# A four-layer graph network on one core: the first layer's softmax scaling moved to GpSimd, and a new order of its steps

## The chip, the core and the metric

The kernel runs on one core of a Trainium2 chip, as one launch. The metric is the device time of a launch in microseconds (us), lower is better. The core has five engines with an instruction queue of their own, which run side by side and wait for one another on semaphores: PE (TensorE, matrix multiplications and transposes, which write the PSUM banks), DVE (VectorE), ACT (ScalarE), POOL (GpSimd, which reads and writes SBUF alone) and SP (SyncE, which here only issues DMAs). Within a queue nothing overtakes: an instruction that waits holds up all that stand behind it.

## The reference

Four graph layers run one after the other over x (128 graphs of 64 nodes, 256 features), each followed by a residual and a layernorm. The change touches the first alone:

```python
    xp = jnp.einsum('mn,bnf->bmf', L_norm, x)
    h = xp @ Wc + bc
    h = _layernorm(h, g1, be1)
    h = jax.nn.relu(h)
    x1 = h + x
    q, k, v = x1 @ Wq, x1 @ Wk, x1 @ Wv          # 4 heads of 64
    scores = jnp.einsum('bhnd,bhmd->bhnm', q, k) / np.sqrt(hd)
    scores = jnp.where(adjacency[None, None] > 0, scores, -1e9)
    attn = jax.nn.softmax(scores, axis=-1)
    o = jnp.einsum('bhnm,bhmd->bhnd', attn, v) @ Wo + bo
    x2 = _layernorm(x1 + o, g2, be2)
    m = jax.nn.gelu(x2 @ W1 + b1) @ W2 + b2
    return _layernorm(x2 + m, g3, be3)
```

## The kernel before

The 8192 tokens are cut into groups of 256 (four graphs, two tiles of 128 rows). Four streams, numbered 0 to 3, work on four groups at a time, each with two PSUM banks and SBUF buffers of its own, and there are 8 turns of four groups. The work on one group is a chain of numbered slots that goes back and forth between the engines. A step is written s.n below: 3.11 is slot 11 of stream 3. A slot can have a part on more than one engine.

- 0 and 1: PE mixes the graph's nodes (L288), ACT copies, PE multiplies by Wc (L889); DVE adds the bias (L808) and takes layernorm statistics (L353, L357).
- 1 on POOL: reciprocal standard deviation (L365, L367). 2 on DVE: the layernorm's two passes (L395, L400), ReLU and residual (L815).
- 3: PE transposes (L921), ACT and DVE split the value in two (L675, L798). 4 and 5: PE makes q, k (24 matmuls of L332) and v (12 of L332), which ACT copies out (L678, L681, L684).
- 6: PE makes the scores (L952, L962), DVE their negated maximum (L819). 7: ACT takes the exponential (L688). 8: DVE sums (L823), takes the reciprocal (L825) and multiplies (L827).
- 9: PE transposes the weights (L969), ACT copies (L693). 10: PE weights v (L980), ACT copies (L696). 11: PE multiplies by Wo (L889), DVE adds the residual (L832) and takes statistics (L353, L357), POOL the reciprocal deviation (L365, L367). 12 on DVE: the two layernorm passes (L395, L400).
- 13 to 15 and 150: transposes (L921), the MLP up (L332), gelu on ACT (L705), down (L913), and DVE's add and statistics (L841). 16 on DVE: the third layernorm; 17 on DVE and POOL: statistics of the last one; 18: ACT applies it, SP stores.
- 3, 13 and 16 on POOL: a bias is added in four pieces of 128 x 128 each, by the helper at L301.

Which of these stands where in an engine's queue comes from a table written by hand, `plan0`: for each engine a tick for each slot, a period of 88 ticks, and for each stream a lead. The function `weave` walks the ticks of a period and issues what is due; it sets only the order, since the queues run as fast as their semaphores allow. In the profile's names PSUM is `ps`, most SBUF buffers lie in `H`, and PE's fp32 matmuls are counted twice (a product of 4 instructions is a row with x8, a transposition of 4 one with x4).

Of the kernel before, what the change touches and what calls it, by code (L numbers as in the profile page):

```python
# [21 lines left out]
ALU = mybir.AluOpType  # L22
# [5 lines left out]
P = 128  # L28
BATCH, NODES, D = 128, 64, 256
# [88 lines left out]
def build_program(nc, ctx, t, out_rows):  # L118
# [107 lines left out]
    bc, g1, be1, bo, g2, be2, b2, g3, be3 = (vec0[:, n, :] for n in range(9))  # L226
# [66 lines left out]
    PIECES = 4  # L293
# [54 lines left out]
    LN_STATS = 2 * TILES - 1  # L348
# [40 lines left out]
    LN_AFFINE = 2 * TILES  # L389
# [124 lines left out]
    def half_blocks(h):  # L514
# [2 lines left out]

    plan0 = dict(
        period=88, lead=(0, 12, 20, 32),
        pe={0: 13, 1: 20, 3: 29, 4: 36, 5: 40, 6: 45, 9: 59, 10: 60, 11: 67, 13: 75, 14: 82, 15: 89, 150: 91},  # L520
        act={0: 17, 3: 32, 4: 39, 5: 42, 7: 53, 9: 60, 10: 63, 13: 79, 14: 86, 18: 167, 140: 87},
        dve={1: 25, 2: 27, 3: 34, 6: 49, 8: 57, 11: 72, 12: 72, 13: 79, 15: 97, 16: 106, 17: 153},
        pool={1: 19, 3: 41, 11: 63, 13: 77, 15: 96, 16: 70, 17: 150},
        sp={2: 42, 4: 0, 18: 116})

    with nc.Block() as block:

# [50 lines left out]
        def _(pool):  # L578
# [11 lines left out]
            c = Chain(pool, pool_steps)  # L590
# [47 lines left out]
            def stage(s, slot, turn):  # L638
                for n, at in enumerate((1, 11)):
                    if slot == at:  # L640
                        ln_reciprocal(pool, steps.enter(s, slot, turn), s, var_ready[s], rstd_ready[s],
                                      2 * turn + n + 1)
                if slot == 15:
                    ln_reciprocal(pool, tail.enter(s, slot, turn), STREAMS + s, var2_ready[s], rstd2_ready[s],
                                  2 * turn + 3)
                if slot == 17:
                    ln_reciprocal_and_shift(pool, tail.enter(s, slot, turn), STREAMS + s, var2_ready[s],
                                            rstd2_ready[s], 2 * turn + 4)
                if slot == 3:
# [63 lines left out]
        def _(dve):  # L713
# [69 lines left out]
            for k in range(KD):  # L783
# [2 lines left out]
            dve.sem_inc(late_made, 1)  # L786
            dve.wait_ge(w0_loaded, 16 * 16)

            steps = Steps(dve, "l0_dve", {1: 1 + LN_STATS, 2: LN_AFFINE, 8: 2, 11: 1 + LN_STATS,
                                          12: LN_AFFINE - 1})  # L790
            tail = Steps(dve, "l0_dve_tail", {15: 1 + LN_STATS, 16: LN_AFFINE - 1, 17: LN_STATS})
            ahead(dve, var2_ready, by=2)
# [8 lines left out]
            def stage(s, slot, turn):  # L801
                c = (steps if slot < 15 else tail).enter(s, slot, turn)
                for n, (at, h) in enumerate(((3, 0), (13, 1))):
                    if slot == at:
                        split_lo(s, FM * turn + n + 1, h)
                if slot == 1:
                    dve.wait_ge(product_done[s], 3 * turn + 1)
                    c.step(dve.tensor_tensor(hb_t[s], token_major(s, 1), over_tiles(bc), ALU.add))  # L808
                    c.settle()
                    ln_statistics(dve, c, hb_t[s], s, var_ready[s])  # L810
                if slot == 2:
                    c.step(ln_affine(dve, c, hb_t[s], s, g1, lambda n: be1, var_ready[s], rstd_ready[s], 2 * turn + 1))
                    c.settle()
                    dve.wait_ge(xs_loaded[s], 16 * turn + 16)
                    dve.scalar_tensor_tensor(out=x1_t[s], in0=hb_t[s], scalar=0.0, in1=xs_t[s],  # L815
                                             op0=ALU.max, op1=ALU.add).then_inc(x_ready[s], 1)
                if slot == 6:
                    dve.wait_ge(sc_done[s], turn + 1)
                    dve.tensor_reduce(sm_max[:, s, :].rearrange("p (b c) -> p b c", b=2), score_blocks(s), AX_X,  # L819
                                      ALU.max, negate=True).then_inc(sc_ready[s], 1)  # L820
                if slot == 8:
                    dve.wait_ge(exp_ready[s], turn + 1)
                    c.step(dve.tensor_reduce(sm_sum[:, s, :], attn[s], AX_X, ALU.add))  # L823
                    c.settle()
                    c.step(dve.reciprocal(sm_inv[:, s, :], sm_sum[:, s, :]))  # L825
                    c.settle()
                    dve.tensor_tensor(attn[s], attn[s], sm_inv[:, s, :].unsqueeze(2).to_broadcast([P, 2 * NJ, NODES]),  # L827
                                      ALU.mult).then_inc(at_ready[s], 1)
                if slot == 11:
                    dve.wait_ge(product_done[s], 3 * turn + 2)  # L830
                    dve.wait_ge(biased_ready[s], 2 * turn + 1)
                    c.step(dve.tensor_tensor(hb_t[s], token_major(s, 0), x1b_t[s], ALU.add))  # L832
                    c.settle()
                    ln_statistics(dve, c, hb_t[s], s, var_ready[s])
                if slot == 12:
                    ln_affine(dve, c, hb_t[s], s, g2, lambda n: be2, var_ready[s], rstd_ready[s], 2 * turn + 2)\
                        .then_inc(x_ready[s], 1)
                if slot == 15:
                    dve.wait_ge(product_done[s], 3 * turn + 3)
                    dve.wait_ge(biased_ready[s], 2 * turn + 2)  # L840
                    c.step(dve.tensor_tensor(y_t[s], token_major(s, 0), x2b_t[s], ALU.add))  # L841
                    c.settle()
                    ln_statistics(dve, c, y_t[s], STREAMS + s, var2_ready[s])
                if slot == 16:
                    dve.wait_ge(xb_ready[s], turn + 1)
                    ln_affine(dve, c, y_t[s], STREAMS + s, g3, lambda n: xr0_t[s][:, n, :], var2_ready[s],
                              rstd2_ready[s], 2 * turn + 1, 2 * turn + 3).then_inc(y_made[s], 1)
                if slot == 17:
                    dve.wait_ge(y_made[s], turn + 2)
                    ln_statistics(dve, c, y_t[s], STREAMS + s, var2_ready[s])  # L850
                (steps if slot < 15 else tail).leave(s, slot)
# [1141 lines left out]
```

## Time and profile before

| | us |
|---|---|
| median of 3 runs | 2195.67 (2194.35 to 2195.98) |
| the profiled execution, its own time | 2193.9 |
| its span | 2192.0 |
| a turn of the first layer, steady | 72.96 |
| PE busy in that turn | 72.58 |
| DVE / ACT / POOL busy in that turn | 63.28 / 37.81 / 42.14 |

The first layer takes about the first 640 us of the span. Its loop begins at 32.8 us and PE's last matmul in it ends at 626.1 us; the next layer's first starts at 645.9 us. The time outside the span (1.9 us) is launch and end. A row of the timeline gives start, duration, engine, line, operation, output and input, and in brackets how long the engine had stood idle and for whom.

### The profile page before, as it was taken

What the parts mean: (1) busy time and instruction counts of PE and PEld (TensorE: products, weight loads), DVE (VectorE), ACT (ScalarE), POOL (GpSimd) and SP (SyncE); (2) the same over time, 40 slices, a digit from 0 to 9 for tenths busy, and PEclk for the clock granted to TensorE, in tenths of its full rate; (3) what the DMA queues carried; (4) which work ended last, traced back from release to release, by engine and by line L of the source; (5) the groups of instructions that cost most, each with busy time, mean ns of one, the idle gap of its engine ahead of it and who ended that gap; (6) DMA issues with size and microseconds to landing.
All of it is one profiled execution on the core that took longest, in us unless ns stands there. A gap on an engine that the chain in (4) does not pass through costs nothing. (4 is left out here: it accounts for less than half of the span.)

```text
span 2192.0 us, 44070 instructions
## 1 busy us (share of the span) xinstructions
PE 2105.3 (96%) x17941; PEld 1843.1 (84%) x17941; DVE 1368.7 (62%) x2737; ACT 1158.0 (53%) x2184; POOL 472.8 (22%) x1131
## 2 busy tenths in 40 slices
PE   6999999999969989999999999999999999899998
PEld 4899889988959978888888999988888799777886
DVE  5788888888866644433334443353444488876775
ACT  1554465445534457644445444353443477657987
POOL 3555565556530000000000000000000122003343
PEclk9999999999989999999999999999999999999999
DMA  4001211121131110000000000000000143001333
GB/s 128 16 21 50 59 36 35 49 59 37 36 109 58 57 51 20 1 20 1 1 1 20 20 1 1 1 0 20 1 1 1 47 125 121 1 20 45 83 88 78
DMA packets 77074, 82.99 MB, mean 38 GB/s; under 512 B 7136, under 2 KB 74592, under 8 KB 76000
## 3 DMA queue, kind: packets, MB, share of 16 engines
q1 hardware_dynamic: 76896, 80.53, 12.4%
q8 instruction: 122, 2.00, 0.4%
q14 instruction: 56, 0.46, 0.1%
HBM read 55.34 MB, written 25.17 MB: 37 GB/s over the span
## 5 line engine op out<-in xcount | busy, mean ns | idle before, releaser
L332 PE MATMUL ps<-R 128*128 128x256 f32 (+3 forms) x8136 | 1489.9, 343 | 12.1 <-DVE R L1461 7.4
L332 PEld LDWEIGHTS ps<-R 128*128 128x128 f32 x8136 | 1308.6, 190 | 169.6 <-issue 7.5
L1407 ACT ACTIVATE late_half<-ps,lstm_bias 128x512 f32<-128x512 f32 (+2 forms) x460 | 283.0, 669 | 375.3 <-PE ps L332 375.3
L374 POOL TENSOR_TENSOR ln_veps<-ln_mv,eps_tile 128x2 f32<-128x2 f32 x128 | 24.9, 195 | 1179.2 <-DVE ln_mv L357 1179.2
L301 POOL TENSOR_TENSOR H<-H 128x128 f32<-128x128 f32 x384 | 203.8, 563 | 1.4 <-DMA residual<-H 1.4
L1477 DVE TENSOR_TENSOR late_half<-late_half 128x1024 f32<-128x1024 f32 (+2 forms) x32 | 37.6, 1176 | 183.6 <-ACT late_half L1407 183.6
L1401 ACT ACTIVATE late_half<-late_half 128x1024 f32<-128x1024 f32 (+2 forms) x66 | 68.1, 1031 | 125.0 <-DVE late_half L1482 78.5
L889 PE MATMUL ps<-H 128*128 128x256 f32 x512 | 125.3, 388 | 0.8 <-ACT H L672 0.8
L913 PE MATMUL ps<-H 128*128 128x256 f32 x512 | 120.3, 380 | 0.0
L1479 DVE TENSOR_TENSOR late_half<-late_half 128x1024 f32<-128x1024 f32 (+2 forms) x32 | 37.6, 1176 | 131.1 <-ACT late_half L1407 131.1
L400 DVE SCALAR_TENSOR_TENSOR H<-H,ln_rstd 128x256 f32<-128x256 f32 x192 | 99.3, 557 | 13.4 <-POOL ln_rstd L367 11.4
L889 PEld LDWEIGHTS ps<-H 128*128 128x128 f32 x512 | 94.5, 194 | 12.3 <-ACT H L672 1.0
L913 PEld LDWEIGHTS ps<-H 128*128 128x128 f32 x512 | 94.7, 190 | 12.0
L1489 DVE TENSOR_TENSOR H<-late_half 128x1024 f32<-128x1024 f32 (+2 forms) x34 | 45.9, 1350 | 89.8 <-ACT late_half L1407 89.8
L353 DVE BATCH_NORM_STATS2 ln_stats<-H 128x6 f32<-128x256 f32 x256 | 95.8, 415 | 3.3
L1461 DVE TENSOR_TENSOR R<-H,R 128x1024 fp32r<-128x1024 f32 (+2 forms) x66 | 95.7, 1451 | 1.3 <-ACT R L1380 1.1
L1380 ACT ACTIVATE R<-H 128x1024 fp32r<-128x1024 f32 (+2 forms) x66 | 94.4, 1431 | 0.0
L395 DVE SCALAR_TENSOR_TENSOR H<-H,ln_mv 128x256 f32<-128x256 f32 x192 | 90.1, 509 | 1.6
L377 POOL TENSOR_TENSOR ln_rstd<-ln_veps,minus_half 128x2 f32<-128x2 f32 x128 | 88.5, 692 | 10.0
L1492 DVE TENSOR_TENSOR late_half<-late_half 128x1024 f32<-128x1024 f32 (+2 forms) x32 | 37.6, 1176 | 80.8 <-ACT late_half L1407 80.8
L1475 DVE TENSOR_TENSOR late_half<-late_half 128x1024 f32<-128x1024 f32 (+2 forms) x34 | 40.9, 1202 | 58.6 <-ACT late_half L1407 58.6
L357 DVE BATCH_NORM_AGGREGATE ln_mv<-ln_stats 128x2 f32<-128x6 f32 x448 | 55.7, 165 | 33.8 <-DVE ln_stats L353 1.5
(213 smaller groups left out, 2547.4 us busy)
## 6 DMA issues: line engine op xcount, KB each, us to landing
H<-in_x SPq DMA_DIRECT2D x64, 256.0 KB, 3.0
residual<-H SPq DMA_DIRECT2D x32, 256.0 KB, 2.2
H<-residual SPq DMA_DIRECT2D x32, 256.0 KB, 3.8
arena<-residual SPq DMA_DIRECT2D x32, 256.0 KB, 2.9
residual<-arena SPq DMA_DIRECT2D x32, 256.0 KB, 2.1
H_state<-residual SPq DMA_DIRECT2D x32, 256.0 KB, 2.9
out<-H_state SPq DMA_DIRECT2D x64, 128.0 KB, 2.4
arena<-in_wih SPq DMA_DIRECT2D x4, 1024.0 KB, 4.9
```

What stands on the lines that cost most here:

```text
L301: ins = pool.tensor_tensor(out[:, n, f:f + words], in0[:, n, f:f + words], in1[:, n, f:f + words], ALU.add)
L332: mm = pe.matmul(out, lhsT(a), rhs(b), start=start and n == 0, stop=stop and n == len(PASSES) - 1)
L353: c.step(dve.bn_stats(ln_stats[:, s, n, :], y[:, n, :]))
L377: c.step(pool.tensor_tensor(ln_rstd[:, s, :], ln_veps[:, s, :], minus_half[:, 0:TILES], ALU.pow))
L395: c.step(dve.scalar_tensor_tensor(out=y[:, n, :], in0=y[:, n, :], scalar=ln_mv[:, s, n, 0:1], in1=g, op0=ALU.subtract, op1=ALU.mult))
L400: ins = dve.scalar_tensor_tensor(out=y[:, n, :], in0=y[:, n, :], scalar=ln_rstd[:, s, n:n + 1], in1=be_of(n), op0=ALU.mult, op1=ALU.add)
L889: mm = pe.matmul(out[:, n, :], src[:, k, n * P:(n + 1) * P], w[:, k, :], start=(k == 0), stop=(k == blocks - 1))
L913: mm = pe.matmul(out[:, n, :], src[:, k, n * P:(n + 1) * P], W2[:, k, :], start=n == 0 and k == 0, stop=n == TILES - 1 and k == HID0 // P - 1,
L1380: act.activation(x.operand_window(xin[x.s][:, 0]), x.window(), ACT.Copy).then_inc(x_hi[x.s], 1)
L1401: act.activation(x.part(bg), x.part(cell[s]), ACT.Tanh).then_inc(tanh_ready[s], 1)
L1407: ins = act.activation(into[q][:, m, 0:x.cols], gate_ps(q, m, x.cols), ACT.Tanh if q == TANH_G else ACT.Sigmoid, bias=lstm_bias[:, x.p - 1 ...
L1461: dve.tensor_tensor(x.operand_window(xin[x.s][:, 1]), x.window(), x.operand_window(raw(xin[x.s][:, 0])), ALU.subtract).then_inc(x_ready[x. ...
```

## The change

The multiplication of the softmax weights by the reciprocal sums leaves DVE. It is done by POOL in a new slot 8 of its own, in four pieces of 128 x 128; DVE's part of slot 8 ends with the reciprocal, which now raises `var_ready`. All five rows of the table of ticks are new.

```diff
     plan0 = dict(
         period=88, lead=(0, 12, 20, 32),
-        pe={0: 13, 1: 20, 3: 29, 4: 36, 5: 40, 6: 45, 9: 59, 10: 60, 11: 67, 13: 75, 14: 82, 15: 89, 150: 91},
+        pe={0: 7, 1: 13, 3: 24, 4: 30, 5: 33, 6: 41, 9: 55, 10: 61, 11: 63, 13: 73, 14: 82, 15: 83, 150: 88},
...
-        sp={2: 42, 4: 0, 18: 116})
+        sp={2: 11, 4: 22, 18: 130})
...
                 for n, at in enumerate((1, 11)):
                     if slot == at:
                         ln_reciprocal(pool, steps.enter(s, slot, turn), s, var_ready[s], rstd_ready[s],
-                                      2 * turn + n + 1)
+                                      3 * turn + 2 * n + 1)
+                if slot == 8:
+                    pool.wait_ge(var_ready[s], 3 * turn + 2)
+                    for piece in range(PIECES):
+                        j = slice(2 * NJ // PIECES * piece, 2 * NJ // PIECES * (piece + 1))
+                        ins = pool.tensor_tensor(attn[s][:, j], attn[s][:, j],
+                                                 sm_inv[:, s, j].unsqueeze(2).to_broadcast([P, 2 * NJ // PIECES, NODES]),
+                                                 ALU.mult)
+                    ins.then_inc(at_ready[s], 1)
...
                     c.step(dve.tensor_reduce(sm_sum[:, s, :], attn[s], AX_X, ALU.add))
                     c.settle()
-                    c.step(dve.reciprocal(sm_inv[:, s, :], sm_sum[:, s, :]))
-                    c.settle()
-                    dve.tensor_tensor(attn[s], attn[s], sm_inv[:, s, :].unsqueeze(2).to_broadcast([P, 2 * NJ, NODES]),
-                                      ALU.mult).then_inc(at_ready[s], 1)
+                    dve.reciprocal(sm_inv[:, s, :], sm_sum[:, s, :]).then_inc(var_ready[s], 1)
```

The changed kernel's lines are numbered from 5 to 8 higher from the first edit on: L889 is L894 there, L921 L926, L969 L974, L832 L837, L823 L831, L825 L833, and the new multiplication is L647. The digit behind a semaphore's name is the stream.

First place: PE's queue from slot 11 of stream 3 (`mixed_ready3`) to slot 13 of the same stream (`x_ready3`). Before:

```order
L889 MATMUL ps<-H2,H 128x256 [waits mixed_ready3]
L889 MATMUL ps<-H2,H 128x256 x3
L332 MATMUL ps<-R 128x256 [waits fm_ready0]
L332 MATMUL ps<-R 128x256 x23
L969 MATMUL ps<-ident,H2 128x128 [waits at_ready2]
L969 MATMUL ps<-ident,H2 128x128 x3
L332 MATMUL ps<-R 128x256 [waits qkv_ready0]
L332 MATMUL ps<-R 128x256 x11
L980 MATMUL ps<-H2,H 64x64 [waits atT_ready2]
L980 MATMUL ps<-H2,H 64x64 x15
L921 MATMUL ps<-ident,H 128x128 [waits x_ready3]
L921 MATMUL ps<-ident,H 128x128 x3
```

And in the changed kernel:

```order
L894 MATMUL ps<-H2,H 128x256 [waits mixed_ready3]
L894 MATMUL ps<-H2,H 128x256 x3
L332 MATMUL ps<-R 128x256 [waits qkv_ready0]
L332 MATMUL ps<-R 128x256 x11
L974 MATMUL ps<-ident,H2 128x128 [waits at_ready2]
L974 MATMUL ps<-ident,H2 128x128 x3
L957 MATMUL ps<-mask0,ident_r 128x256 [waits qkv_ready0]
L957 MATMUL ps<-mask0,ident_r 128x256
L967 MATMUL ps<-H2 64x64 x16
L985 MATMUL ps<-H2,H 64x64 [waits atT_ready2]
L985 MATMUL ps<-H2,H 64x64 x15
L926 MATMUL ps<-ident,H 128x128 [waits x_ready3]
```

Stream 0's 24 matmuls of slot 4 left the stretch (they stand ahead of it now), and stream 0's scores, slot 6, came in: only slot 9 of stream 2 stands between them and slot 5 now.

Second place: DVE's queue over the same stretch, from the residual add of 3.11 (`product_done3`) to the second layernorm pass of 3.12 (`rstd_ready3`). Before:

```order
L832 TENSOR_TENSOR H<-ps,H 128x512 [waits biased_ready3,product_done3]
L353 BN_STATS ln_stats<-H 128x6 [waits l0_dve3]
L353 BN_STATS ln_stats<-H 128x6
L357 BN_AGGR ln_mv<-ln_stats 128x2 [waits l0_dve3]
L357 BN_AGGR ln_mv<-ln_stats 128x2
L395 SCALAR_TENSOR_TENSOR H<-H,ln_mv,H2 128x256 [waits var_ready3]
L395 SCALAR_TENSOR_TENSOR H<-H,ln_mv,H2 128x256
L400 SCALAR_TENSOR_TENSOR H<-H,ln_rstd,H2 128x256 [waits rstd_ready3,l0_dve3]
L400 SCALAR_TENSOR_TENSOR H<-H,ln_rstd,H2 128x256
L823 TENSOR_REDUCE sm_sum<-H2 128x8 [waits exp_ready1]
L825 RECIPROCAL sm_inv<-sm_sum 128x8 [waits l0_dve1]
L827 TENSOR_TENSOR H2<-H2,sm_inv 128x512 [waits l0_dve1]
```

In the changed kernel:

```order
L837 TENSOR_TENSOR H<-ps,H 128x512 [waits biased_ready3,product_done3]
L353 BN_STATS ln_stats<-H 128x6 [waits l0_dve3]
L353 BN_STATS ln_stats<-H 128x6
L357 BN_AGGR ln_mv<-ln_stats 128x2 [waits l0_dve3]
L357 BN_AGGR ln_mv<-ln_stats 128x2
L831 TENSOR_REDUCE sm_sum<-H2 128x8 [waits exp_ready1]
L833 RECIPROCAL sm_inv<-sm_sum 128x8 [waits l0_dve1]
L395 SCALAR_TENSOR_TENSOR H<-H,ln_mv,H2 128x256 [waits var_ready3]
L395 SCALAR_TENSOR_TENSOR H<-H,ln_mv,H2 128x256
L400 SCALAR_TENSOR_TENSOR H<-H,ln_rstd,H2 128x256 [waits rstd_ready3,l0_dve3]
L400 SCALAR_TENSOR_TENSOR H<-H,ln_rstd,H2 128x256
L827 TENSOR_REDUCE sm_max<-ps 128x8 [waits sc_done0]
```

The sum and reciprocal of stream 1 moved in between the statistics of 3.11 and the passes of 3.12; the multiplication is gone.

Third place: DVE's queue in front of slot 8 of stream 3, in the changed kernel. The four rows that wait for and follow `y_made3` (slot 17 of the turn before) stood behind 2.6 there before, further down:

```order
L816 TENSOR_TENSOR H<-ps,H2 128x512 [waits product_done0]
L353 BN_STATS ln_stats<-H 128x6 [waits l0_dve0]
L353 BN_STATS ln_stats<-H 128x6
L357 BN_AGGR ln_mv<-ln_stats 128x2 [waits l0_dve0]
L357 BN_AGGR ln_mv<-ln_stats 128x2
L353 BN_STATS ln_stats<-H 128x6 [waits y_made3]
L353 BN_STATS ln_stats<-H 128x6
L357 BN_AGGR ln_mv<-ln_stats 128x2 [waits l0_dve_tail3]
L357 BN_AGGR ln_mv<-ln_stats 128x2
L831 TENSOR_REDUCE sm_sum<-H2 128x8 [waits exp_ready3]
L833 RECIPROCAL sm_inv<-sm_sum 128x8 [waits l0_dve3]
L395 SCALAR_TENSOR_TENSOR H<-H,ln_mv,H2 128x256 [waits var_ready0]
```

So the sum of 3.8 stands one slot later in DVE's queue than it did. On PE, slot 5 of stream 1 (12 matmuls of L332) moved ahead of 3.9, behind which it stood. On POOL, slot 8 of each stream stands behind the reciprocal deviation of another stream: 3.8 behind 0.1, 1.8 behind 3.11. The first and the last steps of every queue but SP's, those of 3.0 to 3.3 in the first turn and those from 0.14 and 0.15 on in the last, stand as they did.

## Rows read from the trace of the kernel before

**Rows 1.** The page: span, and busy time by engine.

```profile
span 2192.0 us, 44070 instructions
PE 2105.3 (96%) x17941; PEld 1843.1 (84%) x17941; DVE 1368.7 (62%) x2737; ACT 1158.0 (53%) x2184; POOL 472.8 (22%) x1131
```

**Rows 2.** Busy time of each engine in one turn, with PE's granted clock.

```profile
core 0: us, PE busy (x) PEld busy (x) DVE busy (x) ACT busy (x) POOL busy (x), PEclk, DMA share, GB/s
319.42:392.38 72.96, 72.58 (x810) 65.56 (x809) 63.28 (x152) 37.81 (x90) 42.14 (x88) 1.00 0.15 45
```

**Rows 3.** All waits of PE from 33 to 640 us.

```profile
PE ps L921 <- DVE H L815: 4.6, 1, 4.6
PE ps L288 <- DVEq L62: 3.0, 1, 3.0
PE ps L969 <- DVE H L827: 1.8, 8, 0.2
PE ps L889 <- ACT H L672: 0.8, 1, 0.8
```

**Rows 4.** Timeline of PE, a turn's stretch from 1.6 to 1.9.

```profile
363.23 1.99 PE L889 MATMUL ps<-H 128*128 128x256 f32 x8
364.87 3.22 PE L332 MATMUL ps<-R 128*128 128x256 f32 x24
367.93 0.60 PE L969 MATMUL ps<-ident,H 128*128 128x128 f32 x4
368.28 1.68 PE L332 MATMUL ps<-R 128*128 128x256 f32 x12
369.89 0.69 PE L980 MATMUL ps<-H 64*64 64x64 f32 x32
370.63 0.66 PE L921 MATMUL ps<-ident,H 128*128 128x128 f32 x4
371.38 0.50 PE L952 MATMUL ps<-mask,ident_r 128*128 128x256 f32 x2
371.82 0.69 PE L962 MATMUL ps<-H 64*64 64x64 f32 x32
372.74 0.66 PE L969 MATMUL ps<-ident,H 128*128 128x128 f32 x4 [0.23 <-DVE H L827]
```

**Rows 5.** Timeline of DVE over the same stretch.

```profile
364.74 0.69 DVE L823 TENSOR_REDUCE sm_sum<-H 128x8 f32<-128x512 f32 x1 [0.35 <-ACT H L688]
365.46 0.20 DVE L825 RECIPROCAL sm_inv<-sm_sum 128x8 f32<-128x8 f32 x1
...
366.31 0.68 DVE L832 TENSOR_TENSOR H<-ps,H 128x512 f32<-128x512 f32 x1
...
368.20 0.91 DVE L395 SCALAR_TENSOR_TENSOR H<-H,ln_mv 128x256 f32<-128x256 f32 x2
...
369.37 1.21 DVE L400 SCALAR_TENSOR_TENSOR H<-H,ln_rstd 128x256 f32<-128x256 f32 x2 [0.26 <-POOL ln_rstd L367]
```

**Rows 6.** Timeline of ACT, the copy of 0.5; and two passes of L400 elsewhere.

```profile
370.67 0.66 ACT L684 ACTIVATE H<-ps 128x512 f32<-128x512 f32 x1
...
352.83 0.88 DVE L400 SCALAR_TENSOR_TENSOR H<-H,ln_rstd 128x256 f32<-128x256 f32 x2
```

**Rows 7.** Timeline of all engines around 3.8 and 3.9.

```profile
356.09 0.69 DVE L823 TENSOR_REDUCE sm_sum<-H 128x8 f32<-128x512 f32 x1
...
357.11 5.03 POOL L301 TENSOR_TENSOR H<-H 128x128 f32<-128x128 f32 x8
...
358.19 0.40 PE L952 MATMUL ps<-mask,ident_r 128*128 128x256 f32 x2
...
359.14 0.66 PE L969 MATMUL ps<-ident,H 128*128 128x128 f32 x4
...
361.52 0.73 DVE L353 BATCH_NORM_STATS2 ln_stats<-H 128x6 f32<-128x256 f32 x2
...
363.11 0.69 DVE L798 TENSOR_TENSOR R<-ps,R 128x512 fp32r<-128x512 f32 x1 [0.45 <-ACT R L675]
```

**Rows 8.** POOL's pieces (min/median/max ns), four of them undisturbed, and averages by group.

```profile
L301 POOL TENSOR_TENSOR H<-H x288: 446/460/943, 112.5 to 544.3; 128x128 f32<-128x128 f32 x144
...
620.26 1.70 POOL L301 TENSOR_TENSOR H<-H 128x128 f32<-128x128 f32 x4 [1.37 <-DMA residual<-H]
...
L301 POOL TENSOR_TENSOR H<-H 128x128 f32<-128x128 f32 x288 | 153.2, 564 | 0.0
...
L827 DVE TENSOR_TENSOR H<-H,sm_inv 128x512 f32<-128x512 f32 x24 | 17.5, 731 | 0.8
```

More of the change, by code:

```diff
@@ L519, in build_program @@
         period=88, lead=(0, 12, 20, 32),
-        pe={0: 13, 1: 20, 3: 29, 4: 36, 5: 40, 6: 45, 9: 59, 10: 60, 11: 67, 13: 75, 14: 82, 15: 89, 150: 91},
-        act={0: 17, 3: 32, 4: 39, 5: 42, 7: 53, 9: 60, 10: 63, 13: 79, 14: 86, 18: 167, 140: 87},
-        dve={1: 25, 2: 27, 3: 34, 6: 49, 8: 57, 11: 72, 12: 72, 13: 79, 15: 97, 16: 106, 17: 153},
-        pool={1: 19, 3: 41, 11: 63, 13: 77, 15: 96, 16: 70, 17: 150},
-        sp={2: 42, 4: 0, 18: 116})
+        pe={0: 7, 1: 13, 3: 24, 4: 30, 5: 33, 6: 41, 9: 55, 10: 61, 11: 63, 13: 73, 14: 82, 15: 83, 150: 88},
+        act={0: 14, 3: 27, 4: 34, 5: 37, 7: 48, 9: 58, 10: 63, 13: 76, 14: 84, 18: 162, 140: 86},
+        dve={1: 23, 2: 27, 3: 33, 6: 50, 8: 58, 11: 76, 12: 78, 13: 87, 15: 99, 16: 107, 17: 144},
+        pool={1: 9, 3: 39, 11: 62, 13: 83, 15: 89, 16: 83, 17: 137, 8: 47},
+        sp={2: 11, 4: 22, 18: 130})
     with nc.Block() as block:
@@ L787, in _ @@
             dve.wait_ge(w0_loaded, 16 * 16)
-            steps = Steps(dve, "l0_dve", {1: 1 + LN_STATS, 2: LN_AFFINE, 8: 2, 11: 1 + LN_STATS,
+            steps = Steps(dve, "l0_dve", {1: 1 + LN_STATS, 2: LN_AFFINE, 8: 1, 11: 1 + LN_STATS,
                                           12: LN_AFFINE - 1})
@@ L811, in stage @@
                 if slot == 2:
-                    c.step(ln_affine(dve, c, hb_t[s], s, g1, lambda n: be1, var_ready[s], rstd_ready[s], 2 * turn + 1))
+                    c.step(ln_affine(dve, c, hb_t[s], s, g1, lambda n: be1, var_ready[s], rstd_ready[s], 2 * turn + 1, 3 * turn + 1))
                     c.settle()
@@ L835, in stage @@
                 if slot == 12:
-                    ln_affine(dve, c, hb_t[s], s, g2, lambda n: be2, var_ready[s], rstd_ready[s], 2 * turn + 2)\
+                    ln_affine(dve, c, hb_t[s], s, g2, lambda n: be2, var_ready[s], rstd_ready[s], 2 * turn + 2, 3 * turn + 3)\
                         .then_inc(x_ready[s], 1)
```

## The prediction, on record before the changed kernel was run

> **What bounds the kernel now.** I read the page first, to see which engine is full: PE works 2105 of 2192 us, POOL 473 [rows 1]. Only the first layer is touched, so next came the busy time of one of its turns, between two starts of slot 0 of stream 3: PE 72.58 of 72.96 us at the full clock of 2.4 GHz (share 1.00), DVE 63.3, POOL 42.1 [rows 2]. So PE is the bound, and its work is not changed: the same matmuls stand in another order. What a change can win or lose here is time in which PE stands still. The list of PE's waits holds four rows [rows 3]. Three occur once, in the first turn, and stand before steps whose order is the same in the new table. The fourth, 1.8 us over 8 times, is the transposition of softmax weights waiting for DVE's multiplication, which the change replaces. So I looked at the timeline of PE around it [rows 4].
>
> The reader should see there how little room there is. A matmul block ordinarily begins 0.07 to 0.36 us before the end of the one ahead: L332 begins at 364.87, L889 ends at 365.22. At three places it doesn't. The transposition of 3.13 begins at 370.63, 0.05 after the end of L980 (370.58). The scores of 0.6 begin at 371.38, 0.09 after 371.29. That of 1.9 begins at 372.74, 0.23 after 372.51. Counted from the overlap that such a block has elsewhere (0.07 after 64-wide blocks, 0.16 after 128-wide ones), these are 0.12, 0.25 and, with 0.16, 0.39 us: **0.76 us of standing still in a turn, 6.1 us in eight**. That is all that a better order could win in the steady turns.
>
> **The change, part by part.** (a) DVE loses the multiplication, 0.731 us each, 32 in all; POOL gains four pieces for each. Nothing on the trace multiplies on POOL by a broadcast; the nearest row is the bias add in pieces of the same 128 x 128, 0.564 us on average, 0.425 with DVE out of the way (1.70 for four), 0.943 at worst [rows 8]. Four pieces so cost 1.7 to 3.8 us, 2.26 by the mean. POOL's turn grows from 42.1 to 51.2 us of 73; it does not become the bound. DVE's shrinks by 2.9 at most. Neither is PE's time, so the busy times cost nothing; what counts is whether the weights are ready later than PE wants them.
>
> On this the Trainium skill speaks against the change: its page GPSIMD Engine Reference, section 4.1 Engine selection, sends elementwise work to VectorE and puts GpSimd at about twice its time for two inputs. The rows show 2.26 against 0.73, three times, and not twice. By the page's factor the four pieces would take 1.46 us, and (c) below would add nothing; the sum would be the same but for that.
>
> (b) **The stretch from 3.11 to 3.13.** PE's new order puts 0.5, 2.9, 0.6 and 2.10 between the two. From the starts of consecutive rows, 3.11 takes 1.64 us, 0.5 takes 1.61, 2.9 takes 0.35, 2.10 at most 0.74 (I take 0.70, some of it is the wait just named) [rows 4], and a scores block 0.95 (358.19 to 359.14) [rows 7]. Together 5.25 us. Before, the 24 matmuls of 0.4, 3.06 us (364.87 to 367.93), stood there, and not the scores.
>
> What 3.13 waits for: the product ends 1.99 us after its start; DVE's add starts some 0.05 later and its chain (add, statistics, two passes around POOL's deviation) took from 366.31 to the transposition at 370.63, 4.32 us [rows 4, 5]. That is 6.36 us already, more than the 5.25 of room. Before, DVE came 1.09 late to it (366.31 against 365.22) and there was still only 0.12 of standing still, since there was more PE work between. The new order also puts sum and reciprocal of 1.8 between statistics and passes: 0.72 (364.74 to 365.46) and 0.20, together 0.92, of which 0.26 falls into the idle time that DVE had before L400 [rows 5]. So 0.66 more: **7.02 us of chain against 5.25 of work, 1.77 us of standing still in each turn**. A first part of it falls before 0.6: its copy of v takes 0.66 on ACT [rows 6] after matmuls that end 0.07 after the next block's time (1.68 against 1.61), and only 0.35 of PE work covers it [rows 4], 0.4 us. It is not in addition; it uses up the same slack. Bounds: the passes of L400 took 1.21 us there with POOL's pieces beside them, 0.88 where POOL is idle [rows 5, 6]. In the new order the pieces of 1.8 run just then, so 1.21 is the nearer row; with 0.88 the stall is 1.44.
>
> (c) **1.9 and 3.9 behind POOL.** Counting from the start of 3.11: DVE's statistics are done at 2.04 + 1.89 (366.31 to 368.20) = 3.93, sum and reciprocal of 1.8 at 4.85, POOL starts about 4.95. Its pieces beside DVE's passes go at 0.63 (5.03 for eight, [rows 7]), so 2.52, done 7.47. PE would reach 1.9 at 7.02 + 0.35 = 7.37. Wait 0.1; with undisturbed pieces none, and the 0.39 that 1.9 waited before is gone. For 3.9: DVE's sum started at 356.09; now slot 17 stands ahead, 1.14 us (361.52 to 363.11 less 0.45 idle), so 357.23, plus 0.92 makes 358.15, POOL from 358.25 to 360.77. PE comes there at 359.14 + 1.61 for the twelve matmuls of 1.5 = 360.75 [rows 4, 7]. Wait 0 to 0.1. Both are on the edge: each 0.1 us more per piece costs up to 0.4 us at each place.
>
> (d) SP's table, moved far: loads now stand before stores of streams 0 to 2. The loads are a turn ahead of their use, and a store is waited for by POOL's 13 alone, which has a whole turn less some steps; covered by PE's 73 us of other work, I put it at nothing. If the cover failed, POOL's 13 and then DVE's 15 would be late, and the next slot 0 with them. ACT's order changes little; its exponentials still stand together, ahead of the gelus, so no table load is added. The first turn's start and the last turn's end have the same order on every engine that matters: nothing.
>
> **Sum**, against the profiled execution's own 2193.9 us. Per turn + 1.77 (b) less 0.76 that it replaces is + 1.01, times 8 is + 8.1; with L400 undisturbed (1.44) + 0.68, times 8 is + 5.4. (c) adds 0 to 1.6. I take + 7.5, nearer the first: 2201.4. The median of the runs shown is 1.8 above the profiled one, so a median of **2203 us**.
>
> **Rivals.** A measurement of this kernel tells about 0.2%, 4.4 us, from no change.
>
> *No measurable change.* For it: the stall only has to be 1.1 us instead of 1.77. This is so if sum and reciprocal of 1.8 hide wholly in DVE's wait (0.66 less): + 0.35 a turn, + 2.8 us, 2198.5. Against: the rows have 0.26 of idle time there and not 0.92.
>
> *POOL late at 1.9 and 3.9.* If a multiplied piece costs 0.75 us (half way from 0.564 to the worst, 0.943), four take 3.0: 0.5 us more at each place, + 1.0 a turn, + 8 on the forecast, 2211. It decides from about 0.63 a piece on. For it: the pieces of 3.8 run beside DVE's passes of 0.2, and the worst pieces are beside such instructions. Against: the mean is 0.564. The Trainium skill, GPSIMD Engine Reference, section 1 Specifications, says why there are such pieces: SBUF interfaces shared with VectorE where that has two SBUF inputs. The trace agrees, with 446 to 943 ns for one shape.
>
> *Faster.* All three places of now are freed and no new one comes: 0.76 less a turn, 6.1 us, 2189.6. It needs the chain of (b) to fit into 5.25 us, that is 1.8 us less than the rows give, or PE to come late to 3.11 relative to DVE so that the order of waits is another; DVE's 2.9 us of relief a turn and the wider room of 3.9 (1.61 more) and 0.9 speak for it. It turns at 3.13: with a stall there under 0.76 the change gains. Against it: 6.36 us of bare chain.
>
> **How the numbers follow.** The forecast has 52 in 100, POOL late 16, no measurable change 26, faster 6. Slower by over 0.2% is 52 + 16 = 68, within 26, faster 6. The range leaves out the faster case and the lower third of the no-change case (under + 1.3), some 14, and the top of the POOL case, 6: 2197 to 2213.
>
> **What would show it.** In the changed kernel: a turn of about 74 us; in PE's waits a row of the transposition L926 for DVE's L400, some 0.8 to 1.4 us eight times (the rest before the scores L957, for ACT's copy of v, L692); the 1.8 us of L974 gone or now for POOL's L647, under 0.2 each; pieces of L647 between 0.43 and 0.7. I am wrong if a turn is 73.0 or less, if L926 does not wait, or if L974's waits are the large ones.

## The result, and the profile after

The changed kernel takes 2198.66 us (median of 20 runs, 2196.48 to 2202.00), the kernel before 2195.53 (20 runs, 2193.07 to 2197.64): a ratio of 1.0016, 95% interval 1.0010 to 1.0022. It is slower, by about 3.1 us, less than half of the 7.5 that was forecast; that is inside the range of the prediction, below its 2203, and within the 0.2% that it had called no measurable change. The profiled execution took 2198.84 us against 2193.9 before.

The page of the changed kernel, its span and busy time by engine, to be read against [rows 1]:

```profile
span 2196.9 us, 44166 instructions
PE 2101.7 (96%) x17941; PEld 1842.7 (84%) x17941; DVE 1343.4 (61%) x2705; ACT 1159.3 (53%) x2184; POOL 521.4 (24%) x1259
```

The move itself is as announced: 32 instructions fewer on DVE, 128 more on POOL, 48.6 us more of POOL. What wasn't announced: PE is 3.6 us less busy, for the same 17941 matmuls, in a longer span. PE's waits in the first layer (33 to 645 us; against [rows 3]):

```profile
PE ps L926 <- DVE H L400: 8.2, 8, 1.0
PE ps L926 <- DVE H L823: 4.2, 1, 4.2
PE ps L288 <- DVEq L62: 3.1, 1, 3.1
PE ps L957 <- ACT H L692: 2.0, 8, 0.3
PE ps L894 <- ACT H L680: 0.8, 1, 0.8
PE ps L332 <- DVE R L806: 0.2, 1, 0.2
```

The 1.8 us of softmax transpositions is gone, and two rows of eight waits have come: the transposition of 3.13 for the passes of L400, and the scores of 0.6 for ACT's copy of v. The stretch from 3.11 to 1.9, in PE's timeline of the changed kernel (against [rows 4]):

```profile
368.60 1.89 PE L894 MATMUL ps<-H 128*128 128x256 f32 x8
370.14 1.78 PE L332 MATMUL ps<-R 128*128 128x256 f32 x12
371.76 0.60 PE L974 MATMUL ps<-ident,H 128*128 128x128 f32 x4
372.61 0.50 PE L957 MATMUL ps<-mask,ident_r 128*128 128x256 f32 x2 [0.25 <-ACT H L692]
373.04 0.69 PE L967 MATMUL ps<-H 64*64 64x64 f32 x32
373.56 0.65 PE L985 MATMUL ps<-H 64*64 64x64 f32 x32
375.23 0.66 PE L926 MATMUL ps<-ident,H 128*128 128x128 f32 x4 [1.03 <-DVE H L400]
375.73 0.60 PE L974 MATMUL ps<-ident,H 128*128 128x128 f32 x4
376.16 1.89 PE L894 MATMUL ps<-H 128*128 128x256 f32 x8
377.98 0.69 PE L985 MATMUL ps<-H 64*64 64x64 f32 x32
```

3.13 starts 6.63 us after 3.11 (368.60 to 375.23) and stands still for 1.03 of them; 1.9 follows at 375.73 without a wait. DVE's chain over the same time (against [rows 5]):

```profile
370.53 0.69 DVE L837 TENSOR_TENSOR H<-ps,H 128x512 f32<-128x512 f32 x1 [1.49 <-PE ps L894]
371.25 0.75 DVE L353 BATCH_NORM_STATS2 ln_stats<-H 128x6 f32<-128x256 f32 x2
372.15 0.25 DVE L357 BATCH_NORM_AGGREGATE ln_mv<-ln_stats 128x2 f32<-128x6 f32 x2
372.32 0.65 DVE L831 TENSOR_REDUCE sm_sum<-H 128x8 f32<-128x512 f32 x1
373.00 0.20 DVE L833 RECIPROCAL sm_inv<-sm_sum 128x8 f32<-128x8 f32 x1
373.12 0.97 DVE L395 SCALAR_TENSOR_TENSOR H<-H,ln_mv 128x256 f32<-128x256 f32 x2
374.13 1.04 DVE L400 SCALAR_TENSOR_TENSOR H<-H,ln_rstd 128x256 f32<-128x256 f32 x2
```

The sum and the reciprocal of 1.8 do stand between statistics and passes, and L400 no longer waits for the deviation. POOL's pieces of 1.8, and the group of all pieces (min/median/max ns; against [rows 8]):

```profile
373.42 2.02 POOL L647 TENSOR_TENSOR H<-H,sm_inv 128x128 f32<-128x128 f32 x4
...
L647 POOL TENSOR_TENSOR H<-H,sm_inv x128: 400/576/583, 65.9 to 602.6; 128x128 f32<-128x128 f32 x128
```

**Where the time is.** The busy time of the first turn and of a middle one, before and then changed:

```profile
32.79:100.54 67.75, 62.03 (x716) 54.76 (x716) 45.61 (x98) 28.78 (x72) 25.97 (x50) 0.95 0.11 33
```

```profile
32.78:101.78 69.00, 62.52 (x716) 55.38 (x716) 43.62 (x98) 28.93 (x72) 26.46 (x56) 0.95 0.10 32
321.90:395.27 73.37, 71.96 (x809) 65.43 (x808) 60.07 (x148) 37.87 (x90) 48.26 (x104) 1.00 0.14 45
```

A middle turn is 73.37 us against 72.96 [rows 2]: + 0.41. The first turn is + 1.25. With six middle turns (2.5) and the last (+ 0.4) that is 4.1; PE leaves the layer at 630.28 instead of 626.14, and the remaining 0.8 of the span's 4.9 falls into the rest of the program, which the change does not touch. That remainder says nothing of the change: from PE's last matmul in the layer to the end of the span it is 1565.3 us (e7) to 1569.1 (e1) in the eleven traces of this case. Eight turns of + 0.41 are 3.3 us, close to the 3.1 of the medians. In the turn, PE idles 1.41 us (73.37 less 71.96) against 0.38, + 1.03, and is busy 0.62 less.

### The profile page after: what moved, and what is told of

The parts are those of the page before. It is cut to its first block and busy times, and to the rows that moved or that the text cites. A ratio compares the mean times of both kernels' runs of the same rounds, so it can differ in the third digit from the quotient of the medians.

```text
span 2196.9 us, 44166 instructions
## 1 busy us (share of the span) xinstructions
PE 2101.7 (96%) x17941; PEld 1842.7 (84%) x17941; DVE 1343.4 (61%) x2705; ACT 1159.3 (53%) x2184; POOL 521.4 (24%) x1259
## 5 line engine op out<-in xcount | busy, mean ns | idle before, releaser
L332 PE MATMUL ps<-R 128*128 128x256 f32 (+3 forms) x8136 | 1488.8, 343 | 13.3 <-DVE R L1466 7.4
L332 PEld LDWEIGHTS ps<-R 128*128 128x128 f32 x8136 | 1308.8, 190 | 171.4 <-issue 7.9
L301 POOL TENSOR_TENSOR H<-H 128x128 f32<-128x128 f32 x384 | 189.4, 527 | 0.0
L1482 DVE TENSOR_TENSOR late_half<-late_half 128x1024 f32<-128x1024 f32 (+2 forms) x32 | 37.6, 1176 | 183.9 <-ACT late_half L1412 183.9
L894 PE MATMUL ps<-H 128*128 128x256 f32 x512 | 124.7, 387 | 0.8 <-ACT H L680 0.8
L1484 DVE TENSOR_TENSOR late_half<-late_half 128x1024 f32<-128x1024 f32 (+2 forms) x32 | 37.6, 1176 | 131.0 <-ACT late_half L1412 131.0
L894 PEld LDWEIGHTS ps<-H 128*128 128x128 f32 x512 | 95.7, 194 | 12.5 <-ACT H L680 1.0
L400 DVE SCALAR_TENSOR_TENSOR H<-H,ln_rstd 128x256 f32<-128x256 f32 x192 | 97.7, 549 | 9.7 <-POOL ln_rstd L367 7.2
L713 ACT ACTIVATE H<-ps,b_col 128x256 f32<-128x256 f32 x128 | 53.7, 472 | 74.7 <-PE ps L332 74.6
L395 DVE SCALAR_TENSOR_TENSOR H<-H,ln_mv 128x256 f32<-128x256 f32 x192 | 90.5, 512 | 1.0
L1497 DVE TENSOR_TENSOR late_half<-late_half 128x1024 f32<-128x1024 f32 (+2 forms) x32 | 37.6, 1176 | 80.5 <-ACT late_half L1412 80.5
```

Of the source, the lines that this page charges most:

```text
L301: ins = pool.tensor_tensor(out[:, n, f:f + words], in0[:, n, f:f + words], in1[:, n, f:f + words], ALU.add)
L332: mm = pe.matmul(out, lhsT(a), rhs(b), start=start and n == 0, stop=stop and n == len(PASSES) - 1)
L395: c.step(dve.scalar_tensor_tensor(out=y[:, n, :], in0=y[:, n, :], scalar=ln_mv[:, s, n, 0:1], in1=g, op0=ALU.subtract, op1=ALU.mult))
L400: ins = dve.scalar_tensor_tensor(out=y[:, n, :], in0=y[:, n, :], scalar=ln_rstd[:, s, n:n + 1], in1=be_of(n), op0=ALU.mult, op1=ALU.add)
L894: mm = pe.matmul(out[:, n, :], src[:, k, n * P:(n + 1) * P], w[:, k, :], start=(k == 0), stop=(k == blocks - 1))
```

## The experiments

All are compared with the kernel before on the same chip (medians 2195.79 for the first four, 2195.65 for the next three, 2195.13 for the last two). The theory to be tested, A: what decides is the room that PE's order leaves for each chain, and the loss is the chain 3.11 to 3.13, lengthened by the sum of 1.8. The rival, B: the multiplication on GpSimd itself costs the time. A kernel's steady turn is given with its time, since it does not depend on the filling or on the rest of the program.

**e1, the new order, multiplication on DVE as before.**

```diff
-        pool={1: 19, 3: 41, 11: 63, 13: 77, 15: 96, 16: 70, 17: 150},
+        pool={1: 9, 3: 39, 11: 62, 13: 83, 15: 89, 16: 83, 17: 137},
...
```

(The other engines' tables are those of the changed kernel, the code that of before.)

> The new table of ticks, with the multiplication of the softmax weights back on DVE, as before; POOL has no slot 8. Theory A (what costs is room on PE for the chain from 3.11 to 3.13, and DVE's queue in it): the multiplication of 1.8 now stands in that chain too, 0.61 to 0.73 us more in each turn, so PE's wait at 3.13 grows from 1.03 to about 1.7 and the turn from 73.37 to some 74.0; 5 us or more above the changed kernel, about 2204, which is 8 us or more above the kernel before. Theory B (the move to GpSimd is what costs, through slower pieces and shared access, and the order is neutral or good): this kernel is as fast as the one before or faster, 2190 to 2196, and 3.13 waits less than it does in the changed kernel.

Measured: 2211.81 us, ratio 1.0074 (1.0060 to 1.0088). PE's waits in e1:

```profile
PE ps L921 <- DVE H L400: 12.6, 8, 2.2
PE ps L921 <- DVE H L815: 7.8, 8, 4.6
```

B falls here: in this order the move to GpSimd saves 13 us. With the multiplications in DVE's queue the passes reach 3.13 later (a wait of 1.50 a turn instead of 1.03), and slot 3 of stream 0, behind 3.9, waits 0.47 that it does not in the changed kernel. The steady turn is 74.48 us. A had the direction, but its 2204 is 8 us short: it had no wait at slot 3, and none of the clock. In the first turn PE stood idle for 2.16 us before 3.13, and from 82.97 to 86.38 us the granted clock was 0.50. The layer is 9.8 us longer than in the changed kernel; the other 3 us of the 13 lie outside it and are not explained.

**e2, the order before, multiplication on GpSimd.**

```diff
-        pool={1: 19, 3: 41, 11: 63, 13: 77, 15: 96, 16: 70, 17: 150},
+        pool={1: 19, 3: 41, 11: 63, 13: 77, 15: 96, 16: 70, 17: 150, 8: 50},
```

> The old table of ticks, with the multiplication on POOL in four pieces (slot 8 at tick 50 of POOL's row, the rest of the row as before). Theory A: 1.9 and 0.9 had no room in the old order (1.9 stood still for 0.39 us already with 0.73 us on DVE); four pieces of some 0.5 us and a handover more make 1.3 to 1.5 us more at 1.9 and some at 0.9, 10 to 14 us above the kernel before, 2206 to 2210, with the transposition L974 waiting for L647. Theory B' (only the new order costs, the move is free): within 2 us of the kernel before, 2194 to 2198.

Measured: 2212.65 us, ratio 1.0075 (1.0061 to 1.0088). The waits, and a place from the timeline of e2:

```profile
PE ps L974 <- POOL H L647: 13.9, 15, 1.2
...
304.46 0.69 DVE L831 TENSOR_REDUCE sm_sum<-H 128x8 f32<-128x512 f32 x1 [0.21 <-ACT H L696]
305.47 1.47 POOL L647 TENSOR_TENSOR H<-H,sm_inv 128x128 f32<-128x128 f32 x4 [2.19 <-DVE sm_inv L833]
307.00 0.66 PE L974 MATMUL ps<-ident,H 128*128 128x128 f32 x4 [0.90 <-POOL H L647]
```

Here POOL stands idle for the reciprocal, starts at once, and its pieces are at their fastest (0.37 us each). Still 1.9 waits, since PE's order had left room for one instruction of 0.73 us; 0.9 waits too, in seven turns, for 0.82 to 1.16 us. The turn is 74.95 or 75.27 us, and the time lies 2.7 us above A's range. Each half of the change alone costs 16 to 17 us, both together 3: the new order fits the move and not the multiplication on DVE.

**e3, the changed kernel with the four pieces left out on POOL.**

```diff
                 if slot == 8:
                     pool.wait_ge(var_ready[s], 3 * turn + 2)
-                    for piece in range(PIECES):
...
-                    ins.then_inc(at_ready[s], 1)
+                    pool.sem_inc(at_ready[s], 1)
```

> The changed kernel without the multiplication: POOL waits for the reciprocal and at once raises the semaphore of PE's slot 9, so that the softmax weights stay unscaled. It takes all of POOL's pieces out and nothing else. Theory A: the pieces are nearly off the path (no wait of slot 9 is left in the changed kernel); only what they slow DVE's passes of 3.12 by counts, 0.1 to 0.3 us a turn: 1 to 2.5 us less than the changed kernel, 2196 to 2198. Theory B: the pieces are what costs, so this kernel is at least as fast as the one before, 2195.5 or less.

Measured: 2197.74 us, ratio 1.0010 (1.0000 to 1.0019). With no multiplication at all it is 0.9 us from the changed kernel, and not faster than before. (The two intervals overlap, so the times alone don't tell it from the changed kernel.) Its wait at 3.13 and the two passes before it, from the timeline of e3:

```profile
372.34 0.83 DVE L395 SCALAR_TENSOR_TENSOR H<-H,ln_mv 128x256 f32<-128x256 f32 x2
373.21 0.88 DVE L400 SCALAR_TENSOR_TENSOR H<-H,ln_rstd 128x256 f32<-128x256 f32 x2
...
374.14 0.66 PE L921 MATMUL ps<-ident,H 128*128 128x128 f32 x4 [0.72 <-DVE H L400]
```

From the start of L395 to the end of L400 it is 1.75 us here and 2.05 in the changed kernel (373.12 to 375.17): 0.30 is what POOL's pieces of 1.8 cost the passes beside them, and the wait is 0.31 shorter. The turn is 73.07 us, between 72.96 before and 73.37 in the changed kernel. So B is not as strong as it was put, but it is not nothing: 0.30 of the + 0.41 a turn goes away with the pieces.

**e4, the changed kernel without sum, reciprocal and pieces of stream 1.** The part of the chain that is not its own is taken out.

```diff
-                if slot == 8:
+                if slot == 8 and s == 1:
+                    dve.wait_ge(exp_ready[s], turn + 1)
+                    dve.sem_inc(var_ready[s], 1)
...
+                if slot == 8 and s != 1:
```

> The changed kernel without sum, reciprocal and multiplication of slot 8 in stream 1 alone (its weights stay unscaled); the other three streams are whole. It takes out of DVE's queue just what the new order put between the statistics of 3.11 and the passes of 3.12. Theory A: the chain from 3.11 to 3.13 is shorter by the 0.80 us of sum and reciprocal, but POOL's deviation (some 1.1 us, of which the first passes hide 0.97) then comes last, so by about 0.6 to 0.7: PE's wait at 3.13 falls from 1.03 to about 0.4, the turn to about 72.7, 5 us less than the changed kernel: 2193 to 2194, below the kernel before. Theory B: a quarter of POOL's pieces is gone, so a quarter of what they cost, under 1 us: 2198.

Measured: 2194.06 us, ratio 0.9994 (0.9985 to 1.0003), as A had it, though the interval does not tell it from the kernel before. The turn is 72.67 us. PE's wait in e4, and its second pass in 3.12:

```profile
PE ps L934 <- DVE H L400: 3.0, 8, 0.7
...
371.06 0.88 DVE L400 SCALAR_TENSOR_TENSOR H<-H,ln_rstd 128x256 f32<-128x256 f32 x2 [0.26 <-POOL ln_rstd L367]
```

8.2 us has become 3.0, 0.34 a turn, 0.69 less. Not all of that is the sum's. The pieces of 1.8, the very ones that run beside the passes of 3.12, are left out here too, and e3 gives them 0.31. So 0.38 is left for sum and reciprocal: they took 0.68 between the add and the first pass (1.91 us there instead of 2.59), and the second pass now waits 0.26 for POOL's deviation. What is left is the chain of 3.11 to 3.13 itself against 5.1 us of PE work.

**e5, sum and reciprocal of 1.8 behind the passes of 3.12**, on DVE, else as changed.

```diff
+        swap={"dve": [((1, 8), (3, 12))]})
```

(The two neighbours change places in the list of steps; in e6 the same on PE.)

> The changed kernel with one pair of steps exchanged in DVE's queue, in every turn: the passes of 3.12 stand ahead of the sum and reciprocal of 1.8. Nothing is left out. Theory A (a chain has a place where it is late, and making one shorter on a shared queue makes the next late): 3.13 is freed to the same extent as when that sum is left out (its wait falls by 0.6 to 0.7 us), but the sum of 1.8 is now behind 2.1 us of passes and a wait for POOL, so the four pieces for 1.9 end 2 us later, and PE waits 1.5 to 2 us at 1.9 instead: about 8 to 11 us above the changed kernel, 2206 to 2210. Theory C (the place of the sum in DVE's queue was just badly chosen, and the other one is free): 5 us less than the changed kernel, 2193 to 2194, as when that sum is left out.

Measured: 2211.28 us, ratio 1.0069 (1.0055 to 1.0082). Its waits:

```profile
PE ps L983 <- POOL H L656: 13.8, 8, 1.7
PE ps L935 <- DVE H L408: 2.8, 8, 0.3
```

The wait at 3.13 falls to 0.34 (the pieces of 1.8 no longer run beside its passes either), and 1.9 behind it waits 1.73 for POOL. The sum can't stand right behind the passes: it is on the way either to 3.13 or to 1.9. The turn is 74.65 us but for one of 76.24, in which the clock fell at the end of PE's wait of 1.73. PE's busy time and granted clock there:

```profile
309.68:313.09 3.41, 3.33 (x10) 0.50 0.39 132
```

The product of 2.11 took 3.09 us in it instead of 1.89. The trace has two more such stretches, at 84.40 and at 610.05 us. A reckoned without them, and the time lies 1.3 us above its range.

**e6, 1.9 ahead of 3.13 on PE.**

```diff
+        swap={"pe": [((3, 13), (1, 9))]})
```

> The changed kernel with one pair of steps exchanged in PE's queue, in every turn: the transposition of 1.9 stands ahead of that of 3.13. Nothing is left out. In the changed kernel 3.13 began at 375.23 in the profiled turn and POOL's last piece for 1.9 ended at 375.44. Theory A: PE waits for that instead, until about 375.5 where it would have begun 3.13 at 375.23, and 3.13 follows without a wait of its own: 0.2 to 0.4 us more a turn, 2 to 3 us above the changed kernel, 2200 to 2202. Theory C (a step that is ready can be found to fill the wait at 3.13): 1.9 fills 0.44 us of it, 3 us less, 2195.

Measured: 2201.44 us, ratio 1.0027 (1.0017 to 1.0038). One row takes the place of the 8.2:

```profile
PE ps L983 <- POOL H L656: 10.3, 8, 1.3
```

Both chains end within 0.3 us of each other; whichever stands first on PE, the other is then free. The turn is 73.63 us.

**e7, the kernel before with another table**, multiplication on DVE.

```diff
-        pe={0: 13, 1: 20, 3: 29, 4: 36, 5: 40, 6: 45, 9: 59, 10: 60, 11: 67, 13: 75, 14: 82, 15: 89, 150: 91},
+        pe={0: 10, 1: 19, 3: 32, 4: 39, 5: 40, 6: 47, 9: 59, 10: 61, 11: 68, 13: 77, 14: 83, 15: 90, 150: 91},
...
```

> The kernel before, multiplication on DVE, with another table of ticks, near the old one: most entries moved by 1 to 5 ticks so that by the durations of the trace no chain on DVE or POOL is longer than the work on PE in front of it by more than 0.5 us. Theory A (room ahead of each step on PE is what an order is worth): waits of 0.6 and 1.9 stay at about 0.45 and 0.25 us a turn, and the order of block kinds on PE costs less, 3 to 6 us below the kernel before, 2190 to 2193. Rival (the old order is at its best, or what this one gains it loses to slower passes of DVE beside POOL): 2195 or more.

Measured: 2193.14 us, ratio 0.9988 (0.9979 to 0.9997), the fastest of all, 2.5 us under before. That is a little less than A forecast, and the reason that I had given is wrong: its middle turn is 73.13 us, 0.17 longer than before. It gains in the filling. PE's wait before 3.3 in e7, which was 4.6 us in [rows 3]:

```profile
PE ps L921 <- DVE H L815: 1.9, 1, 1.9
```

Its first turn is 59.95 us (before 67.75), its last 91.83 (87.85). The shorter wait is 2.7 of the 7.8 us, and the 4.0 come back at the end. A further part is PE's clock. PE's busy time and granted clock in the filling, before and then in e7:

```profile
38.20:43.30 5.10, 0.63 (x33) 0.80 0.01 3
43.30:48.00 4.70, 4.61 (x16) 0.50 0.19 56
...
38.20:43.30 5.10, 3.90 (x75) 1.00 0.24 84
43.30:48.00 4.70, 3.80 (x24) 1.00 0.21 59
```

Before, PE had next to nothing to do in the first stretch, and the next transposition and product (L921, L889) took 1.12 and 3.62 us at a granted clock of 0.50; in e7 it was at work and at 2.4 GHz, and they took 0.66 and 1.89, 2.2 us less.

**e8, a second table near e7's**, all slots of PE but 0 one to three ticks later, and the other rows moved too.

```diff
-        pool={1: 19, 3: 34, 11: 58, 13: 71, 15: 88, 16: 72, 17: 143},
+        pool={1: 8, 3: 10, 11: 58, 13: 76, 15: 78, 16: 76, 17: 145},
...
```

> Multiplication on DVE as before, another table of ticks near that of e7 (slots 1, 10, 11, 15 of PE one to three ticks later, ACT's exponentials and POOL's adds shifted). In e7 the gain of 2 us lay in the filling: its first turn was 7.8 us shorter than before, its last 4.0 longer, and its steady turn 73.13 against 72.96. If the fill alone decides, this table, which keeps e7's lead of slot 3, gives the same 2191 to 2194. If the steady turn can be brought to 72.6 or less as well (no wait over 0.2 us in PE's list), it gives 2188 to 2191. A PE wait that comes back eight times with 0.5 us or more would make it 2196 or above.

Measured: 2195.80 us, ratio 1.0001 (0.9992 to 1.0010). Neither expectation holds. The fill is as good (1.4 us of that wait), but PE waits for loads of the input, which it does in the first layer of no other kernel here, and the turns grow from 73.07 to as much as 75.04 us:

```profile
PE ps L288 <- DMA H<-in_x: 2.6, 4, 1.2
PE ps L952 <- ACT H L684: 1.8, 8, 0.2
```

Why they come late here, with SP's table unchanged, I have not examined.

**e9, the changed kernel with ticks moved**, in every row but SP's, by 1 to 6.

```diff
-        pe={0: 7, 1: 13, 3: 24, 4: 30, 5: 33, 6: 41, 9: 55, 10: 61, 11: 63, 13: 73, 14: 82, 15: 83, 150: 88},
+        pe={0: 7, 1: 13, 3: 24, 4: 31, 5: 33, 6: 41, 9: 55, 10: 61, 11: 64, 13: 73, 14: 82, 15: 85, 150: 88},
...
```

> Multiplication on GpSimd, the changed kernel's table with single ticks moved (PE 4, 11 and 15 one or two later, DVE's 1, 6, 12, 16 and POOL's 1, 8, 13, 15, 16 by 2 to 6). The theory of room on PE (the chain 3.11 to 3.13 has 6.6 us against 5.1 of PE work, and the move to GpSimd costs nothing beyond its turn) expects that a POOL order without the 1.0 us wait at 3.13 equals the kernel before: 2193 to 2197. The rival, that the four pieces on GpSimd cost time wherever they stand, keeps it at 2198 or above; so would a wait of 0.8 us or more that stays at L926 for DVE's L400.

Measured: 2200.62 us, ratio 1.0024 (1.0015 to 1.0033). The wait of L926 for L400 stays at 8.4 us in 8: the order between 3.11 and 3.13 had stayed too. The turn is 73.67 us. So the condition that A set for its 2193 to 2197 was not met, and this run decides nothing between A and the rival. An order with the multiplication on GpSimd that beats the kernel before was not found.

## Why the prediction was nearly right, and where its number was off

**The mechanism, (b), was right**, place and order of size: 3.13 waits for DVE's L400 eight times, 1.03 shown where 0.8 to 1.4 was forecast, with 0.25 before the scores of 0.6. By e3 and e4 together, 0.31 of the 1.03 is what the pieces of 1.8 do to the passes and 0.38 is the sum of 1.8. (Of the signs that I had named, the turn of about 74 us came as 73.37, and the fastest piece took 0.40 us, under my 0.43.) Standing still between 3.11 and 3.13 was put at 7.02 less 5.25 = 1.77. Measured are 6.63 less 5.12 (1.54 + 1.62 + 0.36 + 0.95 + 0.65) = 1.51. The three terms of the chain that were off:

- The product to DVE's add: 1.93 (368.60 to 370.53) instead of 2.04; the product took its usual 1.89 and not the 1.99 of the row.
- Sum and reciprocal: the way from the add to the first pass grew from 1.89 to 2.59, + 0.70, and from the start of L395 to that of L400 it shrank from 1.17 to 1.01, since L400 no longer waits: 0.54 net instead of 0.66. Some 0.14 of that is the first pass slowed by the pieces (0.97 against 0.83 in e3), so sum and reciprocal come to about 0.40, as e4 has it.
- L400: 1.04 instead of 1.21. I had taken the row disturbed by POOL; the bound with 0.88 is what e3 measures without pieces, and the time lies half way.

**(c) was right**: 1.9 and 3.9 do not wait for POOL. Four pieces took 2.02 us against 2.52, and were done 6.84 after the start of 3.11 instead of 7.47. But e6 shows how narrow it is: 3.13's stall is what hides 1.9's.

**The step that failed is "its work is not changed: the same matmuls stand in another order".** What a block costs PE depends on which block comes next. Eight matmuls of L894 followed by L332 take 1.54 us to the next start (368.60 to 370.14), followed by the 64-wide ones 1.82 (376.16 to 377.98). The block ahead counts as well: the 1.64 that I had used, from one row, is such a product before L332 but behind a 64-wide block [rows 4]. I counted all starts of one turn in both traces, with blocks of the same shape as one kind, and took for each pair of kinds its shortest time: the pairs sum up to 71.23 us before and 70.79 after, so PE's own work is about 0.44 less a turn. The largest parts are one such product that moved from a 64-wide successor to L332 (0.28) and twelve matmuls of L332 (1.5) that stand in one row with others of their kind now, 1.44, and no longer before 64-wide ones, 1.60 (0.16). What stands above the shortest went from 1.73 to 2.58, + 0.85, and 0.85 less 0.44 is the + 0.41 of the turn. (Idle and busy time, + 1.03 and - 0.62, draw the line elsewhere: a stall shorter than the overlap of two blocks counts as busy.) So of the forecast's + 1.01 a turn 0.60 failed to come: about 0.44 by the order of kinds, 0.16 by the smaller stall and the small gaps. This is an account of the two traces, and the 0.44 depends on what is counted as a kind: some groupings give up to 0.6, and one that keeps the transpositions of slot 9 apart gives next to nothing, since it takes some of the stalls for work. No experiment changed the order of kinds alone, so this part is argued and not shown. The turn less the waits that the list shows supports it as far as it goes: 73.37 less 1.28 is 72.09 in the changed kernel, 73.07 less 0.97 is 72.10 in e3, 72.67 less 0.59 is 72.08 in e4, 73.63 less 1.54 is 72.09 in e6, all four with the new order but for a neighbour; before it is 72.96 less 0.23, 72.73. That difference, 0.64, is too large, since the list leaves out stalls shorter than the overlap of two blocks. The prediction counted 0.76 of standing still in a turn of the kernel before, and the same reckoning gives about 1.65 in the changed one. Less these, the turns are 72.20 and 71.72 us, 0.48 apart. (Two terms of that 0.76 were off and cancel: measured by blocks of the same two kinds elsewhere, 0.6 stood still for 0.34 and not 0.25, and 1.9 for 0.30 and not 0.39.)

**"The first turn: nothing" is not refuted.** In the two profiled executions it grew by 0.8 us beyond the turn's own 0.41. Most of it is no wait. Blocks of the filling, before and then changed:

```profile
38.14 0.69 PE L288 MATMUL ps<-lnormT,H 64*64 64x64 f32 x32
47.85 0.76 PE L288 MATMUL ps<-lnormT,H 64*64 64x64 f32 x32
```

```profile
38.40 1.06 PE L288 MATMUL ps<-lnormT,H 64*64 64x64 f32 x32
48.11 1.13 PE L288 MATMUL ps<-lnormT,H 64*64 64x64 f32 x32
```

The same 32 matmuls take 0.76 in one and 1.13 in the other. The granted clock of this stretch, before and then changed:

```profile
48.00:52.20 4.20, 4.20 (x60) 0.99 0.02 4
```

```profile
48.00:52.20 4.20, 4.20 (x57) 0.82 0.02 4
```

PE came back to 2.4 GHz a little later. The third product of the layer so starts 19.50 us after the loop began (52.28 less 32.78), where it was 18.73 (51.52 less 32.79). The other traces show that the new order does not bring this with it. With the new order and the same blocks up to there, the same distance is 18.69 in e9, 18.74 in e4, 18.79 in e1, 18.96 in e3 and e6, and 19.55 in e5; with the order of before it is 19.23 in e2. The block in e9:

```profile
47.99 0.75 PE L288 MATMUL ps<-lnormT,H 64*64 64x64 f32 x32
```

What decides it the traces don't say.

**(a) and (d) were right**: POOL's turn grew to 48.3 us, less than the 51.2 reckoned, and nothing shows in PE's waits for loads or stores. On the move itself: the Trainium skill, GPSIMD Engine Reference, section 4.1 Engine selection, gives GpSimd about twice VectorE's time for two inputs. The rows give more: 4 x 508 ns = 2.03 us against 0.731 [rows 8], 2.8 times, and 4 x 418 = 1.67 in e2, 2.3 times. The Trainium skill, GPSIMD Engine Reference, section 1 Specifications, says that GpSimd shares its SBUF interfaces with VectorE and contends with DVE instructions that have two SBUF inputs. The traces agree: DVE's two passes take 1.75 us in e3, without the pieces, and 2.05 with them.

**Rivals and chances.** The time came out as the rival "no measurable change" had it (2198.5), but not by its reason, the sum wholly hidden: about 0.4 of it was not. Its condition, a stall of 1.1 us, did not occur either: it was 1.51. The range reached down to the result only since it took in two thirds of that rival, so that the time lies inside it is in part luck. I gave the rival 26 in 100 since I had looked only for gains of the chain; a gain of PE's own work was not among my cases.

## What to carry to other kernels

Where one engine is full and executes in a fixed order, price an edit by the distance between two of its instructions against the chain that runs beside them: a slower engine costs little if the order gives it room (here 0.30 us a turn, through the passes that run beside it), and an order laid out for another placement cost 16 us here. Change placement and order together, and look at the filling and at the start-to-start time of each pair of neighbours as well as at the waits: a reordering changes all three. What one place gained stood at once in the next in e5 and e6, so look for what ends second before you move it.

## What was not expected of the hardware

- A block of matmuls takes a time that depends on the kind of the next: 1.54 us before 256-wide fp32r ones and 1.82 before 64-wide ones, for the same eight. Behind a 64-wide block the first was 1.64.
- Four pieces on GpSimd went from 1.47 us (e2, where DVE reduces and takes statistics beside them) to 2.02 (the changed kernel, beside DVE's two-input passes), and those passes from 1.75 to 2.05: both sides pay.
- In the filling, the same 32 matmuls took 0.69, 0.76, 1.06 or 1.13 us, by where PE's clock stood; nine kernels with the same blocks in that stretch came to the third product after 18.69 to 19.55 us.
- A short stall can cost more than itself. After PE had stood idle for 1.73 us the granted clock fell to 0.50, and the turn took 76.24 us instead of 74.65 (e5); other turns of e5 have the same stall and kept the full clock. Work that fills a gap (e7) can win back clock as well as the gap.
